# A fused gated-scan and Hadamard-FFN layer: own step orders per engine in the preparation, a wider low half in one product, and layer norm cut into three steps

## What is computed

```python
xn  = layernorm(x)                                   # x: 2 x 2048 x 512
# attention-like branch: z, xs, B, C, dt = split(xn @ in_proj_w)      (512 x 2192)
xs  = silu(causal_conv1d(xs, conv_w) + conv_b);  B, C = elu(B)+1, elu(C)+1
a   = exp(-softplus(dt + dt_bias) * exp(A_log))
y   = gated linear recurrence over time of (C, B, xs, a), in chunks; y += D * xs
y   = rmsnorm(y) * norm_scale * silu(z)
# FFN branch: fwht is the Walsh-Hadamard transform
h   = fwht(xn * SU_ug);  g = silu(h @ W_gate.T * s1) * (h @ W_up.T * s2)
f   = fwht(g * SU_dp) @ W_down.T * Wscale_dp          # 2048 x 512
out = x + y @ out_proj_w + f
```

## Time and profile before

| what | us |
|---|---|
| median of 3 runs | 2049.78 |
| the profiled execution: its time / its span | 2049.79 / 2047.9 |
| preparation, up to the first product of the block loop | 232.4 |
| one block of the loop (from 697.65 to 811.01) | 113.4 |
| TensorE busy in that block | 111.9 |
| VectorE busy in the first 218 us | 152.6 |

### The profile page before, as it was taken

How to read it: one execution, slowest core, us unless ns; L and a number is a source line. 1 busy time by engine, 2 the same in 40 slices (tenths; PEclk the granted TensorE clock), 3 DMA queues, 4 the chain that set the end, 5 groups by cost and what they waited for, 6 DMA issues and landing times.

```text
span 2047.9 us, 39406 instructions
## 1 busy us (share of the span) xinstructions
PE 1900.1 (93%) x13425; PEld 1331.4 (65%) x13426; DVE 1450.4 (71%) x3226; ACT 979.6 (48%) x2179; POOL 282.9 (14%) x270
## 2 busy tenths in 40 slices
PE   4345699999999999999999999999999999999998
PEld 2122576757676766767676776767676767677675
DVE  5688576767867676767858676767678586767676
ACT  5653453536454453536354444535363544445353
POOL 0000020201103020202102030202011020302020
PEclk8766899999999999999999999999999999999999
DMA  7111112111121202111111202021211112021212
GB/s 294 41 42 41 37 37 52 52 42 52 26 57 36 67 31 52 51 42 51 36 47 36 67 31 73 31 52 52 41 52 34 49 39 65 31 73 31 52 52 51
DMA packets 147857, 107.37 MB, mean 52 GB/s; under 512 B 110030, under 2 KB 111158, under 8 KB 147254
## 3 DMA queue, kind: packets, MB, share of 16 engines
q1 hardware_dynamic: 147238, 105.51, 18.3%
q10 hardware_dynamic: 528, 1.05, 0.2%
HBM read 72.18 MB, written 8.65 MB: 39 GB/s over the span
## 4 chain that ended last, share of the span: by engine, by line
PE 73%; DVE 10%; DVEq 7%; issue 2%; ACT 1%; SPq 0%; DMA 0%; ACTq 0%
PE bank L800 71%; DVE Mx L1173 2%; DVEq L1198 2%; PE bank L867 1%; DVE v L1188 1%; DVE state L1199 1%; DVEq L1083 1%; DVEq L1181 1%; DVEq L1186 1%; DVEq L512 1%; DVEq L1171 1%; DVE rs L1073 1%; DVE tg L1145 1%; DVE xc L1183 1%; DVEq L1146 1%
## 5 line engine op out<-in xcount | busy, mean ns | idle before, releaser
L800 PE MATMUL bank<-xnT,wug 128*128 128x256 f16 x6144 | 707.7, 273 | 0.0
L800 PEld LDWEIGHTS bank<-xnT,wug 128*128 128x128 f16 x6144 | 598.6, 98 | 100.6 <-issue 3.4
L800 PE MATMUL bank<-wd,h 128*128 128x512 f16 x1536 | 362.0, 382 | 0.0
L1049 POOL TENSOR_TENSOR vw<-v,dec 128x512 f32<-128x512 f32 x64 | 77.8, 1215 | 1712.4 <-ACT v L996 1300.2
L959 ACT ACTIVATE tg<-bank,gate_scale 128x256 f32<-128x256 f32 x256 | 118.8, 470 | 305.0 <-PE bank L800 223.0
L800 PEld LDWEIGHTS bank<-wd,h 128*128 128x128 f16 x1536 | 147.1, 98 | 165.7 <-issue 14.5
L800 PE MATMUL bank<-wi,xnT 128*128 128x512 f16 (+1 forms) x1152 | 205.0, 331 | 16.3 <-DMA xnT<-cvx 16.3
L1133 DVE SCALAR_TENSOR_TENSOR cvx<-xc,conv,cvx 128x256 f32<-128x256 f32 x384 | 169.1, 481 | 14.6
L800 PE MATMUL bank<-xnT,wi 128*128 128x256 f16 x1536 | 178.7, 273 | 0.0
L965 ACT ACTIVATE h<-tg 128x256 f16<-128x256 f32 x256 | 102.0, 411 | 143.9 <-PE bank L800 85.5
L800 PEld LDWEIGHTS bank<-wi,xnT 128*128 128x128 f16 x1152 | 101.9, 99 | 105.9 <-issue 19.2
(11 more groups left out here) (236 smaller groups left out, 2468.8 us busy)
## 6 DMA issues: line engine op xcount, KB each, us to landing
Mx<-cs_rows SPq DMA_DIRECT2D x128, 256.0 KB, 3.6
cvx<-in_L_attn_u_dram SPq DMA_DIRECT2D x17, 512.0 KB, 4.9
Mx<-in_L_attn_u_dram SPq DMA_DIRECT2D x16, 512.0 KB, 3.6
out_dram<-Mx SPq DMA_DIRECT2D x16, 512.0 KB, 2.8
wug<-in_L_attn_in_proj_w_dram SPq DMA_DIRECT2D x2, 2048.0 KB, 12.4
big<-in_L_ffn_W_down_dram SPq DMA_DIRECT2D x2, 2048.0 KB, 12.6
pair<-in_L_ffn_W_gate_dram SPq DMA_DIRECT2D x4, 1024.0 KB, 5.2
pair<-in_L_ffn_W_up_dram SPq DMA_DIRECT2D x3, 1024.0 KB, 5.4
```

The lines of the kernel that those rows point to most:

```text
L800: ins = nc.tensor.matmul(out, lhsT, rhs, start=first and n == 0, stop=last and n == len(pairs) - 1)
L1049: pool.tensor_tensor(vw32[:, :].rearrange("p (h d) -> p h d", d=HD), vh, bcast(dec3[:, 1, c, 8 * hf:8 * hf + 8], HD), ALU.mult)
```

## The change

1. `ORDER` goes. `PREP_PE`, `PREP_ACT`, `PREP_DVE` and `PREP_SP` give each engine its own order of the same preparation steps. The first half of `W_down` is loaded before the second group of `W_up` now, and its butterflies are spread between other steps.
2. `dsc` goes: `W_down` is not scaled on VectorE. `dg` makes four diagonal matrices from the scales (in the tile `bc_nat`, once that is free), and the `T` of the 16 down units multiplies by these in place of the identity, as an ordinary f32 product and no longer as a transpose. `dsq` takes the scale in its own instruction.
3. The four tables of the block loop are in another order. `D15` is TensorE's last step of a block now, behind `O1`; stop flags and the wait in `final_sum` follow that.
4. `layer_norm` is cut in `lna` (sums), `lnb` (root), `lnc` (apply), each a step of its own; the load `xin` stands ahead of `bd03` in the sync queue, and `res` ahead of `xd`.
5. `q_low` has 128 rows, the lower 64 of them zero, and `int` multiplies with all 128.

```diff
-bc xp0 F0 xp1 qk cs F1 xp2 G F2 vt0 F3 F4 xp3 vt1 D0 D1 vt2 F5 D2 F6 vt3 int00 D3 F7 itr00 int01 st00 F8 D4 D5
+bc xp0 F0 F1 xp1 F2 qk xp2 cs F3 vt0 F4 xp3 G vt1 D0 F5 D1 D2 vt2 F6 vt3 F7 D3 F8 D4 int00 int01 D5 st00 itr00
...
-PREPARATION = {-1: "sq0 ba0 fs0 bb0", 0: "nq0", 1: "nb0", 2: "nq1", 3: "nb1 nq2", 4: "nb2 nq3", 5: "nb3 nq4", 6: "nb4 nq5", 7: "nb5 ws",
+PREP_DVE = """
+ba0 bb0 nb0 ba1 fs0 bb1 db00 H0 H1 fs1 ba2 H2 bb2 H3 fs2 H4 H5 nb1 ba3 bb3 H6 nb2 fs3 nb3 ba4 nb4 bb4 H7 H8 H9
...
+PREP_SP = """
+wo1 dn0 nat1 in nat2 nat3 nat4 nat5 dn2 nat6 nat7 wo2
...
+            down_diag = [bc_nat[:, :, :].rearrange("p a n -> p (a n)")[:, t * P:(t + 1) * P] for t in range(4)]
...
-                for step in ORDER:
+                for step in PREP_DVE:
...
-                    elif k == "dsc":
-                        dve.wait_ge(down_loaded[n // 2], 16)
-                        nc.vector.tensor_scalar(down_nat[:, n, :], down_nat[:, n, :], down_scale[:, n:n + 1], None, ALU.mult).then_inc(down_scaled, 1)
+                    elif k == "dg":
+
+                        for t in range(4):
+                            ins = nc.vector.tensor_scalar(down_diag[t], ident[:, :], down_scale[:, t:t + 1], None, ALU.mult)
+                        ins.then_inc(diag_made, 1)
...
                         for t in range(4):
-                            ins = nc.tensor.transpose(banks[n % 2][:, t * P:(t + 1) * P], src[:, t, a * P:(a + 1) * P], ident[:, :])
+                            o, block_t = banks[n % 2][:, t * P:(t + 1) * P], src[:, t, a * P:(a + 1) * P]
+                            if n < UG_UNITS:
+                                ins = nc.tensor.transpose(o, block_t, ident[:, :])
+                            else:
+                                ins = nc.tensor.matmul(o, block_t, down_diag[t], start=True, stop=True)
...
-        q_low = sb("q_low", [NS, NT, P], F16)
+        q_low = sb("q_low", [P, NT, P], F16)
...
                         products(o[:, :], [(qK[:, c, :], stateK[:, hf * 512:(hf + 1) * 512]),
-                                           (q_low[:, c, :], stateK[0:NS, hf * 512:(hf + 1) * 512])]).then_inc(ring_filled, 1)
+                                           (q_low[:, c, :], stateK[:, hf * 512:(hf + 1) * 512])]).then_inc(ring_filled, 1)
...
-            def layer_norm(i):
+            def norm_sums(i):
...
+            def norm_root():
...
+            def norm_apply():
...
             def final_sum(i):
                 dve.wait_ge(res_loaded, i * 16)
+                dve.wait_ge(h_used, (i + 1) * KF)
...
+            nc.vector.memset(q_low[:, :, :], 0.0)
```

More of the change, by code:

```diff
@@ L54 @@
 PE_STEPS = """
-bc xp0 F0 xp1 qk cs F1 xp2 G F2 vt0 F3 F4 xp3 vt1 D0 D1 vt2 F5 D2 F6 vt3 int00 D3 F7 itr00 int01 st00 F8 D4 D5
-D6 st01 F9 itr01 F10 z00 F11 D7 itr10 int10 D8 z01 F12 D9 st10 F13 itr11 int11 D10 z10 D11 F14 F15 z11 st11
-D12 D13 D14 D15 O0 O1
+bc xp0 F0 F1 xp1 F2 qk xp2 cs F3 vt0 F4 xp3 G vt1 D0 F5 D1 D2 vt2 F6 vt3 F7 D3 F8 D4 int00 int01 D5 st00 itr00
+D6 F9 F10 D7 st01 itr01 F11 int10 D8 z00 st10 z01 itr10 F12 z10 F13 int11 D9 itr11 D10 z11 F14 F15 D11 O0 D12
+st11 D13 D14 O1 D15
 """.split()
 ACT_STEPS = """
-elu xp0 F0 xb0 qk xp1 xb1 kh F1 sv0 H0 cs F2 xp2 sv1 H1 H2 vt0 xb2 dec00 F3 F4 sv2 xp3 xb3 H3 vt1 dec01 F5 H4
-vt2 sv3 F6 vt3 dec02 H5 H6 dec03 F7 sh00 F8 H7 H8 dec10 dec11 F9 sh01 ssq0 H9 z00 F10 F11 H10 dec12 dec13 z01
-F12 H11 H12 F13 H13 yh00 ssq1 xh0 z10 F14 yh01 F15 sh10 yh10 z11 H14 H15 xh1 yh11 sh11
+elu F0 xp0 xb0 H0 xp1 sv0 F1 xb1 qk F2 H1 kh xp2 H2 sv1 xb2 cs F3 F4 sv2 vt0 xp3 H3 xb3 dec00 H4 F5 vt1 sv3
+dec01 H5 vt2 F6 F7 vt3 H6 dec02 F8 dec03 H7 H8 sh00 dec10 F9 dec11 F10 H9 ssq0 dec12 z00 sh01 dec13 H10 F11
+H11 yh00 z01 F12 yh01 sh10 F13 ssq1 xh0 H12 H13 z10 F14 yh10 z11 xh1 H14 yh11 F15 H15 sh11
 """.split()
 DVE_STEPS = """
[L65 to L68, removed]
+bc fin elu F0 cv0 sv0 F1 L0 cv1 F2 kl L1 qk sv1 cv2 L2 F3 sv2 G F4 L3 cv3 sv3 F5 dec00 L4 L5 dec01 F6 lna lnb
+L6 int00 st00 F7 itr00 F8 int01 dec02 L7 dec03 sl00 F9 lnc L8 itr01 dec10 F10 st01 int10 dec11 L9 ssq0 z00 F11
+sl01 st10 dec12 z01 L10 itr10 dec13 int11 L11 yl00 itr11 F12 yl01 F13 ssq1 L12 z10 F14 yl10 z11 xl0 L13 yl11
+L14 xl1 F15 st11 sl10 L15 sl11
 """.split()
@@ L323, in _ @@
                 act.wait_ge(cols_ready, 1)
-                for step in ORDER:
+                for step in PREP_ACT:
                     k, n = parse(step)
@@ L585, in _ @@
                 pe.wait_ge(negexp_ready, 1)
-                for step in ORDER:
+                for step in PREP_PE:
                     k, n = parse(step)
@@ L837, in body @@
                             ins = products(acc[j][:, :], three(lambda u: h[c % 3][:, u, j * P:(j + 1) * P], lambda u: wd[:, c, u, :]),
-                                           first=c == 0, last=False)
+                                           first=c == 0, last=c == KF - 1 and down_closes(j))
                         ins.then_inc(h_used, 1)
@@ L900, in body @@
                         products(acc[c][:, :], [pq for a in range(CX) for pq in three(lambda u: yT[c][:, a, u, :], lambda u: wo[:, a, u, :])],
-                                 first=False).then_inc(acc_filled, 1)
+                                 first=False, last=not down_closes(c)).then_inc(acc_filled, 1)
             pe.sem_inc(ring_filled, NR)
@@ L1225, in body @@
                         low_xn(i, at[0])
-                    elif k == "ln":
-                        layer_norm(i)
+                    elif k == "lna":
+                        norm_sums(i)
+                    elif k == "lnb":
+                        norm_root()
+                    elif k == "lnc":
+                        norm_apply()
                     elif k == "fin":
```

71 lines of the change are left out of this document (44 added, 27 removed), and 3 rows, old and new, of the table PREPARATION.

## The result

The changed kernel takes 2028.26 us (median of 4 runs, 2026.5 to 2029.5) against 2049.76 for the one before: ratio 0.9895, 95% interval 0.9878 to 0.9912. It is faster by 21.5 us, one per cent. Forecast were 1985 us and a range of 1966 to 2012, so the time lies 43 us above the forecast and 16 above the range. The profiled execution took 2028.65 with a span of 2026.8.

What follows compares the result with a forecast made beforehand. TensorE bounds the loop; VectorE is nearest in the preparation. Span: 2047.9 - 35.3 (preparation) - 13 (q_low) - 14.0 (waits) - 4.9 (half clock) + 3 (F9) = 1983.7, stated as 1985 us of time; range 1966 to 2012.

Steps and rivals of the forecast that it cites:

- At all other places I found TensorE's needs met: Loop, new order: apart from F9, TensorE would get its inputs in time, the L steps within 0.3 us.
- The 14.0 us go: Loop: TensorE's waits before itr10 for dec11 vanish, 14.0 us in 15 blocks, plus 4.9 us of half clock behind them.
- q_low's 13: Loop: with q_low at 128 rows, 64 int pairs each save 0.20 us, 13 us in all.
- rival C: Loop: q_low costs as before, so the pairs gain nothing; 1998 us, chance 0.06.
- The wait before F9: Loop: TensorE waits L - 4.4 us, L being the load for lna, taken as 4.6; 3 us in all.
- Rival D: Loop: late load for lna holds VectorE and TensorE; slower from L = 8.4, or 6.8 with half clock; chance 0.07.
- (b): Preparation: VectorE reaches nb0 at 11 us, but it is ready at about 19; nearly 8 us idle.
- (e): Preparation behind pk: TensorE bounds the tail with 26.7 us of work against VectorE's 19.4; VectorE idles 9 us.
- (a): Preparation: VectorE idles 3 us until the first group lands and before it.
- (c): Preparation: W_down queued before group 1 makes groups 1 and 2 land some 3 us later; 5 us idle counted.
- (f): Preparation: gaps of drained small instructions on VectorE, 3 us.
- Rival A: Preparation gains only a third, its tail behind pk mostly at half clock; 2009 us, chance 0.17.

Runs made afterwards that it cites:

- e9: Changed kernel with the 16 down turns as transposes again and VectorE scaling W_down (dsc): 1995.85 us, ratio 0.9738 to the kernel before.
- e6: Kernel before with only the preparation's new order and the wide q_low; old loop tables, down turns as transposes: 1990.29 us, ratio 0.9715.
- e1: Changed kernel with 64 unused one-column products added at the start of TensorE's program: 2005.74 us, ratio 0.9790 to the kernel before.
- e2: Changed kernel with 128 unused one-column products added at the start of TensorE's program: 2027.93 us, ratio 0.9902 to the kernel before.
- e8: e1 without GpSimd's instructions in the loop, so the state's update and one term are missing: 1987.80 us, ratio 0.9703 to the kernel before.
- e4: Kernel before with q_low at 128 rows as the only change: 2021.33 us, ratio 0.9866.
- e5: Changed kernel with the four loop tables of the kernel before and 64 unused products at TensorE's start: 1996.93 us, ratio 0.9748 to the kernel before.

## Why the prediction was wrong, point by point

**What failed most: a term that the sum does not have.** The part on the preparation priced a down turn as a product at 0.42 us more, "0.86, which is 0.42 more for each of 16 units, 6.7 us of TensorE", and that holds: 0.45 by the rows (0.89 against 0.44), 6.7 and 5.4 us at the first product (e9 and e6). But the sum carried the loop's products over at their spacing of before, as if nothing ahead of the loop could touch it. The same 64 instructions moved the loop to a place where it is fetched again in each block: 22.2 us (e1 against e2), half of the miss of 43. No row of the kernel before shows such a wait, only the queue's row of 9 packets as against 145 after.

**"At all other places I found TensorE's needs met".** Wrong at one place: `dec13` for `itr11`, 8.1 us in 15 blocks. I had laid VectorE's order out with durations from rows in which GpSimd did nothing beside it. e8 shows that these hold only away from GpSimd; without it the same order brings no wait at all.

**"The 14.0 us go" and q_low's 13.** The wait before `itr10` did go, and a pair is 0.43 us, both as forecast. But in e4 the wide `q_low` alone brings 26.5 us, with most of the same wait. With `dec13` and `F9` counted apart the terms do add up (13 + 14.0 + 4.9 - 8.1 - 4.3 = 19.5, and e1's loop is 18.8 shorter), but they were wrong apart: what the order change was credited with is there without it, and itself it costs 9 us (e5 against e1). By the rule that the prediction quotes from the Trainium skill, "TensorE: Matmul & The Clock Gate", part 3 on packing, the term of the pairs would have been 0 (rival C); the pair's 0.43 us speaks against it.

**The wait before F9.** Its place was right, and its size by luck: 0.27 in every block, 4.3 us where 3 were forecast. Rival D needed L = 8.4. The load and VectorE's steps behind it in the changed kernel:

```profile
cvx<-in_L_attn_u_dram SPq DMA_DIRECT2D x2, 512.0 KB, 3.4
```

```profile
705.44 1.29 DVE L1106 BATCH_NORM_STATS2 stats<-cvx 128x6 f32<-128x512 f32 x2 [1.78 <-DMA cvx<-in_L_attn_u_dram]
...
707.12 0.53 DVE L1113 TENSOR_SCALAR rs<-mv 128x2 f32<-128x2 f32 x1
...
709.01 0.68 DVE L1099 SCALAR_TENSOR_TENSOR rs<-rs 128x2 f32<-128x2 f32 x1
```

L is 3.4 and not the 4.6 assumed, so by the formula L - 4.4 there would be no wait. But the tiny steps of 0.17 and 0.16 us took 0.53 and 0.68 beside GpSimd: a load priced too long and steps priced too short made up for each other. In e8 the gap is gone.

**Preparation.** 25.1 of 35.3 us. Steps (b) and (e) and the late load hold: `nb0` waited 7.66 us, TensorE bounds the tail, the norm starts 2.7 us after the last `H` where 3.1 were forecast. What failed lies ahead of `pk`, which starts at 151.3. By the walk's own terms VectorE has 122.1 us of work there and stands idle for 3 (a) + 8 (b) + 5 (c) + 3 (f) = 19, which gives 141: that is the 10 us. VectorE's waits up to 150 us, the larger ones:

```profile
DVE cmax L549 <- PEq L617: 7.9, 2, 7.7
DVE wug L540 <- ACT wug L370: 3.4, 4, 2.0
DVE pair L425 <- DMA pair<-in_L_ffn_W_gate_dram: 3.3, 1, 3.3
DVE pair L425 <- DMA pair<-in_L_ffn_W_up_dram: 2.7, 2, 1.4
```

VectorE is idle for 29.2 us up to `pk` (151.3 less 122.1 busy), where the walk had 19. The waits that have a row of their own come to 22.7. Of the load waits 1.4 us belong to (a) and 4.6 to (c), for 5 forecast, so these were nearly right. `H` waited 3.4 us for ScalarE where the walk had it covered, two more waits for ScalarE and TensorE (1.4 and 1.2) were not in it, and the small gaps between instructions are 6.5 us in place of step (f)'s 3. Rival A named another reason, half clock in the tail; the granted clock was 0.87 over it.

**The account.** 2028.3 = 1985 + 10.2 (preparation) + 22.2 (fetching) + 8.1 (`dec13`) + 1.3 (`F9`) + 1.5 that I can't place (0.6 of it is that the sum's 1985.6 was stated as 1985).

## What to carry to other kernels

When a change adds or takes instructions ahead of a long loop, look at the instruction queue's packets and at a wait on "issue" behind the loop's jump, and try the same kernel with some idle products more: it costs one line and was worth 1.1% here. Price VectorE's steps by the rows of the place where they will stand; beside GpSimd they may take twice as long. And before you credit a new order with a wait that goes, see what the other parts of the change do to that wait alone.

## What the runs showed of the hardware that was not expected

- A loop of 822 products and as many weight loads goes round without a packet of its instruction queue at one place of the program, and with 9 packets (147 KB) in every block at another, 64 products further on: 22 to 34 us in 16 blocks. At 128 products further it is free again.
- The f32 turn by a diagonal is 8 instructions for four blocks, where the transposes are 4, and takes 0.89 us against 0.44.
- A `tensor_scalar` of 128x512 f32 on VectorE takes 541 ns without GpSimd and 1079 in the mean in the loop beside it; a tiny `scalar_tensor_tensor` of 128x1 takes 160 and 355.
- Where a VectorE and a GpSimd instruction met in e4 and in the kernel before, the one that had begun later took longer: VectorE's 1.28 and 1.38 us in place of 0.69, or GpSimd's 1.55 in place of 1.07.
